# A recurrent layer on one core: PE's early visit to the block of its loop is taken out

## The reference

```python
# x (32, 256, 256) = (batch, time, feature), cond (32, 256)
h = silu(cond @ W1.T + b1)
gate = sigmoid(h @ W2.T + b2)[:, None, :]
# a Haar transform of x along time, every coefficient times gate, and the
# inverse transform; the gate doesn't depend on time, so this is x * gate
x = x + (x + x * gate)
# recurrence over 256 steps, from h0 = cond
h_t = tanh(h_{t-1} @ Wh + x_t @ Wx + b)
out = x + h
```

## Time and profile before

| | |
|---|---|
| median of 3 runs | 197.78 us (197.53 to 198.3) |
| the profiled execution, its own time | 198.18 us |
| its span, first to last instruction | 196.4 us |
| PE busy, share of the span | 176.6 us, 90% |
| DVE busy | 96.8 us, 49% |
| ACT busy | 76.9 us, 39% |
| instructions in the trace | 33590 |

### The profile page before, as it was taken

The page is one execution under the profiler, slowest core; times in us unless marked ns, Lnnn a source line. Parts: engine busy times, 40 slices in busy tenths (PEclk is TensorE's granted clock), DMA queues, the critical chain, the costliest instruction groups (busy, mean ns, idle before and its releaser), DMA issues.

```text
span 196.4 us, 33590 instructions
## 1 busy us (share of the span) xinstructions
PE 176.6 (90%) x16067; PEld 165.3 (84%) x16067; DVE 96.8 (49%) x394; ACT 76.9 (39%) x518; POOL 1.4 (1%) x6
## 2 busy tenths in 40 slices
PE   4789999999999999999999999999999999999995
PEld 2688988988898898888889888888988988898895
DVE  0355465455545545555554554555465455545543
ACT  3134333444433444433444433444433444433442
POOL 2000000000000000000000000000000000000000
DMA  5309999602020020202002020200202020020212
GB/s 191 125 22 325 403 412 409 269 0 107 0 106 3 0 108 0 107 0 106 1 2 107 0 108 0 105 2 2 107 0 107 0 97 12 0 108 0 107 53 53
DMA packets 6861, 17.99 MB, mean 92 GB/s; under 512 B 1470, under 2 KB 2622, under 8 KB 6849
## 3 DMA queue, kind: packets, MB, share of 16 engines
q1 hardware_dynamic: 6384, 17.32, 23.5%
q10 hardware_dynamic: 432, 0.54, 0.8%
q0 software_dynamic: 32, 0.01, 0.0%
HBM read 9.48 MB, written 8.39 MB: 91 GB/s over the span
## 4 chain that ended last, share of the span: by engine, by line
PE 88%; ACT 7%; issue 4%; DVE 0%
PE bank_e L190 48%; PE bank_l L190 39%; ACT h_ring L176 7%; PE bank_e L183 1%; PE gate_bank L190 0%; ACT sig_z L162 0%; DVE silu L340 0%; DVE ones L336 0%
## 5 line engine op out<-in xcount | busy, mean ns | idle before, releaser
L190 PE MATMUL bank_e<-h_ring,wh_sb 128*32 128x32 f32 x4096 | 103.4, 200 | 14.3 <-ACT h_ring L176 14.3
L190 PE MATMUL bank_l<-h_ring,wh_sb 128*32 128x32 f32 x4096 | 99.5, 197 | 0.0
L190 PEld LDWEIGHTS bank_e<-h_ring,wh_sb 128*32 128x32 f32 x4096 | 76.0, 110 | 24.0 <-ACT h_ring L176 21.4
L176 ACT ACTIVATE h_ring<-bank_e 128x32 f32<-128x32 f32 x256 | 50.4, 197 | 111.3 <-PE bank_e L190 111.3
L333 DVE TENSOR_TENSOR x<-x,h_ring 128x128 f32<-128x128 f32 x129 | 37.5, 291 | 86.7 <-ACT h_ring L176 86.7
L190 PE MATMUL bank_l<-x_ring,wx_sb 128*32 128x32 f32 x4128 | 79.9, 199 | 0.0
L190 PEld LDWEIGHTS bank_l<-h_ring,wh_sb 128*32 128x32 f32 x4096 | 77.5, 111 | 0.0
L190 PE MATMUL bank_e<-x_ring,wx_sb 128*32 128x64 f32 x2064 | 74.1, 228 | 0.0
L190 PEld LDWEIGHTS bank_l<-x_ring,wx_sb 128*32 128x32 f32 x4128 | 62.1, 111 | 0.0
L190 PE MATMUL bank_l<-ones,b_sb 128*32 128x32 bf16 x1024 | 53.9, 180 | 0.0
L176 ACT ACTIVATE h_ring<-bank_l 128x32 f32<-128x32 f32 x256 | 50.5, 197 | 0.0
(11 more groups left out here) (31 smaller groups left out, 13.3 us busy)
## 6 DMA issues: line engine op xcount, KB each, us to landing
x<-in_x SPq DMA_DIRECT2D x15, 512.0 KB, 9.5
out_dram<-x SPq DMA_DIRECT2D x15, 512.0 KB, 3.5
x<-in_x SPq DMA_DIRECT2D x1, 384.0 KB, 3.3
w_t<-in_w SPq DMA_DIRECT2D x1, 256.0 KB, 5.0
wx_sb<-in_wx SPq DMA_DIRECT2D x1, 256.0 KB, 5.7
wh_sb<-in_wh ACTq DMA_DIRECT2D x1, 256.0 KB, 5.9
out_dram<-x SPq DMA_DIRECT2D x1, 256.0 KB, 2.4
w_t<-in_w_cond ACTq DMA_DIRECT2D x1, 145.0 KB, 3.3
```

The source lines that it names most:

```text
L176: nc.scalar.activation(h_ring[:, m, s * B:(s + 1) * B], z_of(s, m), ACT.Tanh)\
L190: done = nc.tensor.matmul(out[q:q + 32], weights[:, q:q + 32], moving, start=start, stop=stop, skip_group_check=True)
```

## The change

The visit is taken out: after the warm-up PE goes straight to the gate. The block `pe_visit`, the alignment of that block, the branches to it, back from it and over it go, and the loop's first instruction is put on slot 0 of a block where it was on slot 6. The parameter `columns` of `warm_up` goes with them. Nothing is changed for another engine, and no transfer.

```diff
@@ -217,13 +216,8 @@
             pe.wait_ge(ones_ready, 1)
             warm_up(10)
-            only_pe = bass.OrderedEngineSet([pe.engine])
-            nc.br("pe_visit", engines=only_pe)
-            stage = nc.switch_bb("pe_first_stage")
             for m in range(HALVES):
...
@@ -284,15 +278,7 @@
-            pe.addr_align(bass.FETCH_BLOCK_INSTRUCTIONS, offset=0, max_nops=0)
-            nc.br("pe_loop", engines=only_pe)
-            with nc.body("pe_visit", parent=stage.parent, valid_engines=only_pe):
-                warm_up(1, 32)
-                nc.br("pe_first_stage", engines=only_pe)
-            nc.switch_bb("pe_loop")
-
-
-            with nc.Fori(1, TURNS + 1, engines=only_pe, head_slot={pe.engine: 6}) as turn:
+            with nc.Fori(1, TURNS + 1, engines=bass.OrderedEngineSet([pe.engine]), head_slot={pe.engine: 0}) as turn:
```

More of the change, by code:

```diff
@@ L180, in _, with warm_up @@
         def _(pe):
-            def warm_up(n, columns=256):
+            def warm_up(n):
                 for _ in range(n):
-                    nc.tensor.matmul(idle_ps[:, 0:columns], ones[:], ones[:, 0:1].to_broadcast([P, columns]),
-                                     start=True, stop=True)
+                    nc.tensor.matmul(idle_ps, ones[:], ones[:, 0:1].to_broadcast([P, 256]), start=True, stop=True)
             def by_columns(out, weights, moving, start=False, stop=False):
```

## The result

The changed kernel takes 200.66 us (median of 4 executions, 200.07 to 203.22) against 197.66 us before (4 executions). The ratio is 1.0142, with a 95% interval of 1.0122 to 1.0163 (ratios here leave out executions over 1.5% above the fastest of the same kernel, such as the one of 203.22; the medians hold them). It is slower, as forecast, and by more: +3.0 us against +2.1. The profiled execution took 200.9 us with a span of 199.1, 2.7 more than before; what follows explains this execution, and others of the same kernel lose between 0.7 and 4.4 us (e4).

What follows compares the result with a forecast made beforehand. The prediction took PE to bound the kernel, its loop having no slack for a late start. Stalls of +1.8 us and pace of +0.3 sum to +2.1, forecast 199.9 us by the median, range 198.0 to 202.3.

Steps and rivals of the forecast that it cites:

- The mechanism of the stalls: Loop's first pass: its two blocks are fetched only when needed, so PE stands until 10.6 and from 12.3 to 14.0.
- Two of the forecast's own signs of being wrong: Profile after: first queue 8 packet before 7.2, or slow pace lasting through a whole turn, would count against the forecast.
- The price of a block: Instruction fetch: 1.0 us from request to packet, 2.4 us from packet to first instruction, 3.4 us in all.
- The gain in front: Ahead of the loop: gate at 4.1 instead of 6.10, but loads limit the gain to 0.75 to 1.1 us.
- the two arrivals: Loop's blocks: the first is there at 10.6, the second at 14.0, each 3.4 us after its request.
- The stalls: Loop's first turn: first load past the crossing 1.94 us later, less a swallowed tanh wait of 0.15, so +1.8 us.
- PE's pace: Loop's first turns: half pace after the new idle stretches changes the time by +0.3 us.
- both bounds: Pace term: -0.4 us if already fast at 10.7, +2.4 us if slow for 5.3 us from 14.0.
- The sum: Whole kernel: 1.8 for stalls plus 0.3 for pace, +2.1 us, giving a span of 198.5 us.
- rival 2: One stall: crossing lies before the waits for w2 and b_sb, +0.2 us before pace; 197.5 to 198.4 us, 12%.
- rival 3: Loop's block asked for only at the jump over the padding, at 9.0: 201.7 us, or 204 at 4.7 each; 17%.
- rival 4: Fetches hidden, both blocks in by 9.3 and 11.0, so the kernel gets faster: 196.3 to 197.0 us, 13%.

Runs made afterwards that it cites:

- e4: The changed kernel measured again, unaltered, to see its spread: ten executions from 198.93 to 202.70 us, ratio 1.0099 to the kernel before.
- e1: Kernel before with the visit's branch and matmul kept, but its block in a fetch block of its own behind the loop: 204.18 us, ratio 1.0300.
- e3: Changed kernel with the code behind the warm-up aligned to slot 134, so PE crosses into its second block some 50 instructions earlier: ratio 1.0050 to before.
- e5: Kernel before with a long-fulfilled wait in place of the visit's one matmul: ratio 1.0007.
- e7: Kernel before with a prefetch hint ahead of the warm-up and the visit, a register move for its matmul, behind the gate's first product: ratio 0.9976.
- e11: Kernel before with the load of the rest of x's first chunk cut into turn 1's columns and the others: ratio 1.0005.
- e2: Changed kernel with the loop's head on slot 6, as in the kernel before, still without a visit: ratio 1.0135 to before.
- e8: Changed kernel with 14 warm-up matmuls in front of the loop's jump to cover the first stall: 199.17 us, ratio 1.0062 to before.
- e9: e3 with code from slot 128 and a prefetch hint meant for the loop's second block, its branch never taken: ratio 1.0012 to before.
- e6: Kernel before with the visit put ahead of the warm-up and eight warm-up matmuls left out: 197.17 us against 197.91, ratio 0.9945.
- e10: e6 with the load of the rest of x's first chunk cut into turn 1's columns and the others: ratio 0.9952 to the kernel before.

## Why the prediction was right

**The mechanism of the stalls** was right: the code of the loop is fetched only when PE crosses into its second block and when it enters the loop, PE stands twice for it, and later turns pay nothing. Both stalls came at the places that were forecast. e1, e3 and e5 rule out the other readings of what the visit does; only why the crossing asks for nothing in e1 stays open.

**Two of the forecast's own signs of being wrong** came true. The first packet came at 7.1, before the 7.2 at which two stalls were to be doubted, and yet both stalls followed: the sign took the landing of the bias rows as fixed, and they landed sooner. And the slow pace lasted through a whole turn, turn 2, which by the forecast "makes its term too small". It did.

**The price of a block**, 3.4 us, held. From the crossing at 6.1 the first load was at 9.80 (3.7 us), and from there the second stall ended at 13.08 (3.3 us); in e3 it was 3.0 us from 8.99 to 11.98.

**The gain in front** was mis-sized. The gate started at 3.69 and not 4.1, and the step "the bias needs b_sb (1.55 + 5.5 = 7.05)" took the landing time of before for a fixed one. It landed at 6.0. The first tanh began at 7.51 against 9.85 before, so that 2.3 us were on offer and not 0.75; the stall took all but the 0.67 us by which turn 1 starts sooner. Every profile with a fetch packet between 3.4 and 3.9 us (before, e1, e5, e7, e11) has w2 landing 5.0 to 5.4 us after its issue; those with no packet ahead of 6 us have 3.4 to 3.6 (changed, e2, e3, e4, e8) and 4.0 (e9), and e6 and e10, with their packet at 1.8, have 4.4 and 4.5. So the change also brings the loads in sooner. In the kernel before the bias didn't wait for its rows (it is laid from 7.75, right behind PE's own work); in the changed kernel the earlier landing moved the crossing from 7.2 to 6.1, and the two arrivals that I put at 10.6 and 14.0 came 0.9 us sooner. I had priced the change as if the fetch took nothing from the loads beside it.

**The stalls** therefore cost +0.96 us (13.08 against 12.12 for the first load behind the second stall), not 1.94, or 1.8 less the wait of 0.15. e8, without half pace in the loop, bears the size out with its +0.85.

**PE's pace** was the term that failed. Forecast +0.3, measured +1.83: from the second stall's end to turn 3 it took 6.39 us (13.08 to 19.47), against 4.56 before (12.12 to 16.68). The granted clock had fallen to 0.50 within the stretch of 11 to 13 us, after PE had stood for 2.25 us, worked for 1.2, and stood again for 2.0. I had both bounds right (-0.4 to +2.4) and chose near the wrong one, on the ground that each stretch is shorter than the 2.5 us before 5.85. That ground failed: stretches that short were followed by half pace here and in e4. That it takes two of them, one behind the other, is likely but not shown. The Trainium skill (TensorE: Matmul & The Clock Gate, Part 1) says that idleness halves the clock and sustained work restores it; the rows of the changed kernel agree, with 1.00, 0.50 and 1.00 in turn.

**The sum**: 0.96 + 1.83 = 2.79 us at turn 3, and 2.7 in the span, against 2.1 in the forecast. Two errors of opposite sign, -0.8 and +1.5, made it come out 0.7 us short. That they partly cancel is luck, and so is a part of how near the time lies to the forecast. The term of the pace also isn't one number. By how fast the loads are issued, e8 is at full pace from turn 1 on, e3 is slow until about 12.5 us, e2 until 14.1, e9 until 17.4 and e1 until some time past 21; the changed kernel and e4 are fast in the first half of turn 1 and slow from the second stall until nearly 19 and 18.2. This goes with the spread of 3.8 us in e4. What makes one execution slow for longer than another stays open.

**The rivals.** One stall (rival 2) came true as a kernel of its own: e3 has no first stall. In its profile turn 3 starts at 16.72, as before (16.68). Its ratio of 1.0050 is yet above the range I gave the rival. The mean granted clock is 0.983 to 0.991 in six of its ten executions (199.0 to 200.3 us) and 1.00 in the two fastest (198.1 and 198.2), but also in two of 199.4. Nothing asked for ahead (rival 3) appeared in e1. Of rival 4 nothing was seen.

## What to carry to other kernels

A loop that is entered once and runs in two fetch blocks can lose 2 to 3 us on its first pass (here 2.2 to 3.0 by the medians of two measurements). Look in the trace for "issue" waits that end 2 to 3 us after a packet on the instruction queue starts, and count instructions from the aligned start to find which code the wait falls on. A detour that fetches the blocks in advance pays, but its packet isn't free: ask for it ahead of the first loads (e6) and not among them. Where PE would stand twice in short order, count the half pace that can follow it; in the profiled execution it cost more than the standing (1.83 against 0.96 us).

## What was not expected of the hardware

With one instruction packet of 16 KB, about 1 us long, among the loads, w2's 256 KB landed 1.0 to 2.0 us later (5.0 to 5.4 us against 3.4 to 4.0), and in e7 the later half of the gate's 145 KB 1.9 us later (5.0 against 3.1). Five profiles with it and six without agree, but no run puts such a packet there without a detour or a hint of PE, and how 16 KB take so much isn't shown.

A small difference in asking decides when the packet starts. The branches of e6 and e10, at 0.8 us, had theirs at 1.8; the hint of e7 at 0.9 and the branches at 1.1 (before, e1, e5) had theirs at 3.4 to 3.9. The first loads are issued from 0.73 on.

The printed granted clock doesn't show every stretch of half pace. In e1 turn 2 took 3.97 us, about as long as at a clock of 0.50 (3.96 in e4), but the window prints 1.00:

```profile
18.60:22.50 3.90, 3.63 (x248) 1.00 0.68 196
```

The same holds for the first turn of the kernel before, for turn 1 of e2 and for turn 2 of e9 (3.55 us). The count of loads is the better witness.

From the entry into a block by a jump to the next packet it was 0.6 to 0.9 us (9.7 to 10.4, 8.9 to 9.8), and from a crossing in order, behind a stall, 1.1 (e3: 11.98 to 13.1; e2: 12.47 to 13.6; changed: 13.08 to 14.2), if the end of the stall is taken for the crossing.
